# Moving one pair of maxima products ahead of the first weighing, once per half, in a two-pass softmax attention

## The reference, cut to what matters

```
h = (x - mu) * rsqrt(var + 1e-05) * ln_gamma + ln_beta
qkv = (h @ w_qkv + b_qkv).reshape(B, T, 3, NUM_HEADS, HEAD_DIM)
...
scores = jnp.einsum('bhqd,bhkd->bhqk', q, k) / np.sqrt(HEAD_DIM)
attn = jax.nn.softmax(scores, axis=-1)
out = jnp.einsum('bhqk,bhkd->bhqd', attn, v)
out = out @ w_out + b_out
return residual + out
```

## Time and profile before

| what | value |
|---|---|
| median of three runs | 1149.8 us (1148.0 to 1151.61) |
| the profiled execution's own time | 1148.59 us |
| span of its trace, first to last instruction | 1146.5 us |
| PE busy over the span | 1062.9 us, 93% |
| DVE busy | 997.4 us, 87% |
| ACT busy | 808.4 us, 71% |
| chain that ended last, PE's share | 74% |

### The profile page before, as it was taken

The page is one execution under the profiler, slowest core; times in us unless marked ns, Lnnn a source line. Parts: engine busy times, 40 slices in busy tenths (PEclk is TensorE's granted clock), DMA queues, the critical chain, the costliest instruction groups (busy, mean ns, idle before and its releaser), DMA issues.

```text
span 1146.5 us, 22167 instructions
## 1 busy us (share of the span) xinstructions
PE 1062.9 (93%) x8566; PEld 580.9 (51%) x8566; DVE 997.4 (87%) x1475; ACT 808.4 (71%) x1654; POOL 244.1 (21%) x345
## 2 busy tenths in 40 slices
PE   5997799999999999999999999997899998799995
PEld 4885233333333333333333333334667666788984
DVE  7776999999999999999999999943499988569887
ACT  4452188888888888888888888873578687243443
POOL 6413400000000000000000000102254424565643
PEclk9898599999999999999999999998999998899997
DMA  8595304404423441441343150211133325634321
GB/s 273 155 302 208 51 17 67 67 22 75 68 37 51 67 61 28 76 67 33 55 68 56 39 76 12 92 57 59 39 123 132 117 79 167 194 84 135 103 75 55
DMA packets 87333, 101.55 MB, mean 89 GB/s; under 512 B 21885, under 2 KB 57213, under 8 KB 87229
## 3 DMA queue, kind: packets, MB, share of 16 engines
q1 hardware_dynamic: 86396, 98.56, 36.1%
q10 hardware_dynamic: 832, 1.58, 0.4%
HBM read 55.09 MB, written 43.88 MB: 86 GB/s over the span
## 4 chain that ended last, share of the span: by engine, by line
PE 74%; DVE 8%; ACT 3%; issue 3%; POOL 1%; DMA 1%; SPq 0%; PEldq 0%; ACTq 0%; DVEq 0%; POOLq 0%
PE ps_o L799 25%; PE ps_s L787 19%; PE ps_m L776 10%; PE p_a L1344 3%; DVE maxes L726 3%; PE p_p L1416 2%; PE p_p L1770 2%; PE p_t L1350 1%; PE p_a L1747 1%; DVE zT_lo L2033 1%; PE p_p L1711 1%; ACT L1111 1%; PE p_p L1712 1%; PE p_t L1721 1%; PE p_t L1695 1%
## 5 line engine op out<-in xcount | busy, mean ns | idle before, releaser
L680 ACT ACTIVATE prob<-ps_s 128x512 f32<-128x512 f32 x1024 | 555.8, 597 | 118.1 <-PE ps_s L787 98.3
L726 DVE TENSOR_REDUCE maxes<-ps_m 128x2 f32<-128x1024 f32 x512 | 608.6, 1217 | 17.5 <-PE ps_m L776 14.0
L799 PE MATMUL ps_o<-prob,v_ones 128*32 128x256 f32 x4096 | 327.8, 392 | 8.1 <-issue 7.7
L787 PE MATMUL ps_s<-q_stack,k_stack 64*128 64x512 f32 x1024 | 260.5, 499 | 0.0
L776 PE MATMUL ps_m<-k_stack,q_stack 62*128 62x512 f32 x1024 | 216.6, 416 | 14.8 <-DVE maxes L726 11.1
L787 PEld LDWEIGHTS ps_s<-q_stack,k_stack 64*128 64x128 f32 x1024 | 99.0, 184 | 211.3 <-ACT prob L680 188.3
L799 PEld LDWEIGHTS ps_o<-prob,v_ones 128*32 128x32 f32 x4096 | 81.6, 108 | 196.2 <-ACT prob L680 99.5
L640 POOL COPY v_ones<-v_all 128x512 f32<-128x512 f32 x16 | 9.8, 614 | 528.7 <-PE ps_o L799 528.7
L776 PEld LDWEIGHTS ps_m<-k_stack,q_stack 62*128 62x128 f32 x1024 | 100.9, 192 | 27.5 <-DVE maxes L726 23.4
L407 ACT ACTIVATE p_parts<-ps_qk,cols 128x512 fp32r<-128x512 f32 x32 | 22.0, 687 | 39.8 <-PE ps_qk L452 32.1
L1416 PE MATMUL p_p<-p_hT,w_p 128*128 128x512 f32 x96 | 44.3, 612 | 2.6 <-ACT p_hT L1181 2.6
(11 more groups left out here) (301 smaller groups left out, 1536.9 us busy)
## 6 DMA issues: line engine op xcount, KB each, us to landing
qk_parts<-p_parts SPq DMA_DIRECT2D x32, 512.0 KB, 7.3
q_stack<-qk_parts SPq DMA_DIRECT2D x96, 128.0 KB, 4.7
k_stack<-qk_parts SPq DMA_DIRECT2D x96, 128.0 KB, 7.7
oT<-o_sb SPq DMA_DIRECT2D x32, 256.0 KB, 3.9
x_all<-in_x_dram SPq DMA_DIRECT2D x8, 512.0 KB, 10.1
heads<-oT SPq DMA_DIRECT2D x16, 256.0 KB
inverse<-inverse_sums SPq DMA_DIRECT2D x16, 256.0 KB
out_dram<-x_all SPq DMA_DIRECT2D x7, 512.0 KB, 3.4
```

What stands on the lines that cost most here:

```text
L680: act.activation(prob[at % P_RING][:, h], ps_s[:, (GH * at + h) % S_RING], ACT.Exp, scale=HD ** -0.5).then_inc(exp_done, 1)
L726: dve.tensor_reduce(maxes[:, i // 2, i % 2], ps_m[:, i % M_PAIRS], AX.X, ALU.max).then_inc(m_taken, 1)
L787: pe.matmul(ps_s[:, (GH * (UNITS * slot + KT * qc + kt) + h) % S_RING], r32(k_st[slot][rows, pair, kt * P:(kt + 1) * P]), r32(q_st[slot][r ...
L799: ins = pe.matmul(ps_o[32 * h:32 * h + 32, queries], v_st[slot][:, kt, h], prob[(UNITS * slot + KT * qc + kt) % P_RING][:, h, queries], st ...
```

## The change

In the second unit of a half the pair of products that stood behind the third and fourth score now stands directly behind the first pair of products, ahead of the first weighing. All other units keep their order. Nothing is computed otherwise, and no wait is added to or taken from any instruction.

```
                         for pair in range(2):
                             score(g, u, qc, kt, 2 * pair)
                             score(g, u, qc, kt, 2 * pair + 1)
-                            scores_ahead(g, u, qc, kt, pair, last)
+                            if kt != 1:
+                                scores_ahead(g, u, qc, kt, pair, last)
+                            elif pair == 0:
+                                scores_ahead(g, u, qc, kt, 0, last)
+                                scores_ahead(g, u, qc, kt, 1, last)
                             if last and 2 * (KT * qc + kt) + pair >= OUT_BEGIN:
                                 begin_mixing(2 * (KT * qc + kt) + pair - OUT_BEGIN)
                             weigh_last(g, u, qc, kt, pair, first)
```

## The result

The changed kernel takes 1157.32 us (median of 5 runs, 1155.32 to 1159.96), the kernel before 1149.8 (5 runs, 1148.0 to 1151.78). Run again later beside other kernels it took 1158.3 against 1146.47, 1.0100 (1.0076 to 1.0124). It is slower, by some 0.7 to 1.0%.

A forecast was written before the change was run, and what follows sets the result against it. PE sets the pace, DVE close behind. Thirty halves at 0.21 (6.3 us), 0.5 for the first half and 0.3 for reciprocals make 7.1: 1148.6 + 7.1 = 1155.7, stated as 1156.0 us, range 1152.0 to 1159.5.

The forecast's parts named there:

- What bounds it: In a regular attention half of 20.15 us, PE sets the pace, with DVE only 0.56 us behind it.
- Step 1: Second unit of a half: the moved products wait for DVE's earlier reduction, starting at 401.73 us instead of 401.48.
- Step 2: From the moved products to the first weighing 0.43 us, making it 0.27 late; bounds 0.34 and 0.50.
- the rival with the loads ahead: The moved products' weights load during their hold, so the weighing follows after 0.34 us: +4.4 us, 1153.0; chance 0.10.
- the prediction's paragraph on this: If the moved products' load were pulled ahead, the loss would be 0.11 us smaller a half, about 4 us in all.
- Step 3: Second unit's third and fourth score follow the weighing by 0.57 us, at 402.73 instead of 402.46.
- Step 4: The next unit's second score waits for an exponential until 403.91 us; the products behind it come 0.21 us late.
- absorbed: Exponentials start sooner, so the next unit's second score does not wait: about +1.4 us, 1150; chance 0.09.
- spreading: ACT stays late one unit more, adding a second wait of 0.18 us each half: 5.4 us more, 1161; chance 0.08.
- Step 5: Rest of the half: old order at 1.24 us a half-unit, with no PE gap to give back the 0.21 us.
- the group whose DVE takes reciprocals: Two halves find DVE later and lose up to 0.30 us more each; 0.3 us was added for both.
- the first half: The attention's first half has no copy to wait for, so saves nothing at the weighing: 0.5 us lost, a low estimate.

The follow-up runs named there:

- half reductions: DVE's reductions take maxima over only the first half of their columns, in both kernels: changed kernel 1139.8 us, kernel before 1140.42 us.
- half exponentials: Exponentials take only the first 256 of 512 queries, in both kernels: changed kernel 1146.98 us, kernel before 1137.42 us.

## Why the prediction was right

It said 1156.0 us, from 1152.0 to 1159.5, and slower; measured were 1157.32 and 1158.3. The mechanism is what was right. That the total came so near is in part luck: against the kernel before the medians rose by 7.5 us the first time and by 11.8 the second, and the sum of the traces, at the end of this section, is 2.2 over the forecast's 7.1.

- *What bounds it* was right. PE sets the pace, and DVE, on which nothing waited at this place, became the holder as soon as PE came to it earlier.
- *Step 1, B's hold*: B 0.48 behind A, 0.05 behind the reduction's end, was measured to the hundredth. With the half reductions B is not held and the loss turns into a gain of 0.07 a half: shown.
- *Step 2, 0.43 from B to the weighing*: 405.37 to 405.79, 0.42. The choice between the bounds 0.34 and 0.50, by the last half's rows, was the right one. So the rival with the loads ahead falls: B's load began only with the release, as in the earlier trace rows. The Trainium skill's "TensorE: Matmul & The Clock Gate" (part 2, step by step) says that PE pulls loads of weights ahead of matmuls in flight. A's load was (404.66, 0.23 before its products), and so was B's with the half reductions, where the wait was over in time: all four loads stand in one row from 414.42, and all products in one of 0.64. B's load in the changed kernel, whose wait was not over, was not. In the prediction's paragraph on this, 0.11 a half comes to 3.4 us over 31 halves, where "about 4" was written.
- *Step 3*: third and fourth score at 1.81 behind the first (402.73 - 400.91 = 1.82 said).
- *Step 4, the exponential*: the second score of unit 2 at about 3.00 (403.91 - 400.91 said), and a row of 0.69. Taken away with the half exponentials, 0.17 a half comes back: shown. Both rivals that hung on it, absorbed and spreading, fall: the delay is there, and the half-unit behind it is 1.24 again (408.78 to 410.02). One detail was off: the products behind the late score were said to begin at 404.25, 3.34 behind the first scores, and begin at 407.69, 3.14 behind. Only the second of them and the weighing come late, and the loss is the same.
- *Step 5, nothing gives it back*: 20.36 a half, as written down (20.36).

Two terms of the sum were too small, and are the steps that missed. For the group whose DVE takes reciprocals the prediction added 0.3 for both halves, since DVE held PE back there anyway. Measured: 20.97 against 20.45, 0.52, and 20.67 against 20.17, 0.50, so about 0.30 for each, over the 0.21. In this PE timeline B is held 0.77 behind A, and the longer hold was paid in full:

```profile
690.06 0.50 PE L787 MATMUL ps_s<-q_stack,k_stack 64*128 64x512 f32 x2
690.40 0.39 PE L776 MATMUL ps_m<-k_stack,q_stack 62*128 62x512 f32 x2
691.17 0.50 PE L776 MATMUL ps_m<-k_stack,q_stack 62*128 62x512 f32 x2 [0.38 <-DVE maxes L726]
691.60 0.64 PE L799 MATMUL ps_o<-prob,v_ones 128*32 128x256 f32 x8
```

The 0.30 that this half had over the others before stayed on top; it is another place of the half. And the first half was put at 0.5 and cost 2.08 in this execution (0.7 to 3.5 over the pairs): part of it runs at 1.2 GHz, and the moment of the rise moves too. Summed by the traces, the attention lost 7.07 + 2.08 + 0.16 = 9.3 us against the 7.1 of the prediction, 1.6 of the difference in the first half and 0.3 in the two halves with reciprocals.

## What to carry to other kernels

A matmul moved into another's waiting time brings its own wait along, and that wait stopped everything behind it in PE's order here: before moving work into a gap, look for the semaphore on which the moved work waits, and read when that is released, not whether it was "long done" in the old place. Then look at what stood between two users of a ring of buffers: the pair that was moved away was also the time in which the exponential finished. And a stretch elsewhere in the same program, here the last half without products, can show the new order already, with its price.

## What the runs showed of the hardware

The first half of the attention, in which the granted clock rises from 0.50 to 1.00, took 23.87 us in one execution and 22.74 in another of the same kernel, and 20.70 to 24.22 over the twelve executions of eleven kernels; most regular halves of one kernel repeat to 0.03 us. Of a difference of some 8 us between two kernels, 1 to 2 can be this.

A load of weights that carried an open wait began 0.05 us behind the release (405.32 to 405.37), with its matmul; the same load, its wait over (half reductions), stood in one row with the loads of A, 0.42 from 414.42, and its matmul began some 0.24 behind A's (a row of 0.64 for the four, where a pair has 0.40).
